# A gated recurrent layer with two steps in flight, and cosine attention in two token halves with its routing

## The reference

```python
x = x + cosine_attention(_layernorm(x), ...)   # 8 heads of 8, LayerNorm again inside, q and k scaled to length 1
x = x + moe(_layernorm(x), ...)                # 160 experts, 8 per token, and a shared one
x = x + gated_recurrent(_layernorm(x), ...)
x = x + moe(_layernorm(x), ...)                # the same weights
# then a state-space layer, a mixing layer, rotary attention and the mixing layer again

# gated_recurrent, for norm_inp = rmsnorm(inp, ln_w):
beta = sigmoid(norm_inp @ Wg.T)
hx_hat = norm_inp @ Wc.T
hx = scan over time of  h = (1 - beta) * h + beta * hx_hat
h_norm = rmsnorm(hx, ffn_w)
out = hx + (silu(h_norm @ w1.T) * (h_norm @ w3.T)) @ w2.T
```

## Time and profile before

| | before |
|---|---|
| runs, us | 3164.58, 3166.40, 3166.65 (median 3166.4) |
| profiled execution, us | 3175.44, its span 3173.6 |
| TensorE, VectorE, ScalarE, GpSimd busy, us | 1657.7, 1390.8, 958.2, 1066.0 |
| share of the chain that ended last: TensorE, issue, VectorE, unknown queue, ScalarE | 31%, 18%, 17%, 17%, 12% |
| mean granted TensorE clock | 0.704 of full |

### The profile page before, as it was taken

The page is one execution under the profiler, slowest core; times in us unless marked ns, Lnnn a source line. Parts: engine busy times, 40 slices in busy tenths (PEclk is TensorE's granted clock), DMA queues, the critical chain, the costliest instruction groups (busy, mean ns, idle before and its releaser), DMA issues.

```text
span 3173.6 us, 40197 instructions
## 1 busy us (share of the span) xinstructions
PE 1657.7 (52%) x13844; PEld 1113.4 (35%) x13844; DVE 1390.8 (44%) x3634; ACT 958.2 (30%) x1731; POOL 1066.0 (34%) x1177
## 2 busy tenths in 40 slices
PE   4763113229466633423333294656322456988985
PEld 2552112117344411311222173444211443454454
DVE  3548223213133444744442131334443466676655
ACT  3640000015222312111200042223258833344344
POOL 1003753640344265266336503452562020000001
PEclk9975555559777855555555597778665776898998
DMA  8991111339577611011013296767110000000000
GB/s 243 273 346 35 52 38 50 121 114 380 197 236 221 230 44 38 19 62 41 22 49 118 100 360 210 243 219 247 42 44 20 1 0 1 1 1 1 1 2 28
DMA packets 276792, 352.95 MB, mean 111 GB/s; under 512 B 68624, under 2 KB 161104, under 8 KB 276432
## 3 DMA queue, kind: packets, MB, share of 16 engines
q10 hardware_dynamic: 83984, 153.13, 13.8%
q1 hardware_dynamic: 159840, 130.08, 13.5%
q0 software_dynamic: 32768, 67.17, 6.8%
HBM read 201.35 MB, written 167.51 MB: 116 GB/s over the span
## 4 chain that ended last, share of the span: by engine, by line
PE 31%; issue 18%; DVE 17%; another core or an unknown queue 17%; ACT 12%; DMA 3%; SPq 1%; POOL 1%; ACTq 0%; DVEq 0%; POOLq 0%
ACT arena L1043 5%; PE psum L2159 5%; PE psum L2149 4%; PE psum L2110 4%; PE psum L448 3%; DMA arena<-expert_blocks 2%; PE psum L1494 2%; PE psum L1475 2%; PE psum L432 1%; PE psum L427 1%; ACT arena L1345 1%; PE psum L1491 1%; DVE X L1909 1%; PE psum L1492 1%
## 5 line engine op out<-in xcount | busy, mean ns | idle before, releaser
L1939 POOL DMA_INDIRECT arena<-slot_results,SLOTS x512 | 489.1, 955 | 729.0 <-DMA slot_results<-arena 326.5
L1928 POOL DMA_INDIRECT slot_rows<-arena,SLOTS x512 | 502.4, 981 | 522.2 <-issue 437.2
L1893 DVE COPY arena<-psum 128x512 f32<-128x512 f32 x288 | 195.7, 689 | 827.9 <-remote 521.3
L2149 PE MATMUL psum<-arena 128*64 128x128 f32 x2304 | 224.7, 324 | 299.4 <-issue 288.8
L1982 ACT ACTIVATE arena<-psum 128x512 f32<-128x512 f32 x288 | 172.0, 597 | 679.1 <-remote 304.6
L2159 PE MATMUL psum<-arena 64*128 64x128 f32 x2304 | 239.8, 335 | 206.6 <-issue 130.3
L2159 PEld LDWEIGHTS psum<-arena 64*128 64x128 f32 x2304 | 178.9, 218 | 269.4 <-issue 200.2
L2149 PEld LDWEIGHTS psum<-arena 128*64 128x64 f32 x2304 | 144.9, 158 | 362.8 <-issue 347.3
L2110 PE MATMUL psum<-ident,arena 128*128 128x128 f32 x1152 | 223.1, 325 | 15.7 <-DMA arena<-slot_rows 14.0
L169 POOL TENSOR_SCALAR rstd<-mv 128x4 f32<-128x4 f32 x32 | 6.8, 212 | 637.7 <-DVE mv L581 637.4
L1909 DVE SCALAR_TENSOR_TENSOR X<-arena,WEIGHTS,X 128x128 f32<-128x128 f32 x512 | 179.6, 352 | 27.9 <-DVE X L1909 5.9
(11 more groups left out here) (252 smaller groups left out, 3120.8 us busy)
## 6 DMA issues: line engine op xcount, KB each, us to landing
arena<-slot_rows ACTq DMA_DIRECT2D x288, 256.0 KB
slot_results<-arena ACTq DMA_DIRECT2D x288, 256.0 KB
arena<-expert_blocks SPq DMA_DIRECT2D x512, 96.0 KB
slot_rows<-zeros SPq DMA_DIRECT2D x2, 18432.0 KB, 79.9
arena<-own_blocks SPq DMA_DIRECT2D x44, 256.0 KB
slot_rows<-arena,SLOTS POOLq DMA_INDIRECT x512
arena<-slot_results,SLOTS POOLq DMA_INDIRECT x512
expert_blocks<-in_expert_w SPq DMA_DIRECT2D x1, 7680.0 KB, 26.1
```

Source lines behind the costliest of these rows:

```text
L1893: dve.tensor_copy(YSB[:, p].rearrange("p (c h) d -> p h c d", h=2), psum[:, first:first + 2, 0:256].rearrange("p h (c d) -> p h c d", c=2) ...
L1928: pool.indirect_dma_start(out=slot_rows[h], out_offset=bass.IndirectOffsetOnAxis(ap=slots_of(t, k), axis=0), in_=XNH[:, t], in_offset=None ...
L1939: pool.indirect_dma_start(out=GATHERED[:, n % TPI, k], out_offset=None, in_=slot_results[h], in_offset=bass.IndirectOffsetOnAxis(ap=slots_ ...
L2149: mm = pe.matmul(psum[lo:lo + INTER, 2 + 5 * (p % 2), o:o + P], gate_of(g, q), XSBT[:, p % 2, P * q:P * q + P], start=True, stop=True, ski ...
```

## The change

It has two parts. In the first, the attention runs in two halves of 16 tiles (4 steps each), and each half is followed by its routing: attention 0, routing 0, attention 1, routing 1. So the dispatch of half 0 stands beside the second half of the attention. For that the steps are written out (no loop), the barrier between the layers is gone, the padded copies and the inverse deviation move from GpSimd to VectorE (with ScalarE's Sqrt), the buffers lie elsewhere, and the first buffer is cleared ahead of the copies of the expert weights, the second behind them, with a semaphore each. In the second part, the recurrent layer has two steps in flight: the scan of step i + 1 and the front of step i + 2 stand ahead of step i's gates. The root mean square is no longer a full 128x512 tile but four columns (L660's reciprocal becomes one of 4 columns); `ffn_w` is multiplied into the weights once, the two products with W1 and W3 become eight of 128x128 that take the state itself, and a transposition and a copy are added. Sigmoid becomes Tanh and Abs, Sigmoid times its argument becomes Silu. The row sums are distributed anew.

```diff
         def middle_vector(dve):
...
-            own_tiles(dve)
             for h in range(HALVES):
+                cos_vector(dve, 0, HSTEPS * h, HSTEPS * h + HSTEPS)
+                if h == 0:
+                    own_tiles(dve)
+                dve.wait_ge(loaded_all, 16 * (len(weights) - FIRST_WEIGHTS))
                 route_half(dve, 0, h, nothing)
                 slots(dve, 0, h)
...
-        SUMS = ((0, 1), (2, 3, 4), (5, 6), (7, 8, 9))
+        SUMS = ((0,), (1, 2), (3, 4), (5,))
+        ROUTE_SUMS = ((6, 7), (8, 9), (10,), (11, 12))
...
                 for t in range(TPI):
                     place(dve, 1, t)
                 rows_of_slots(dve, 1, 0)
-                glru_front(dve, GLRU_AHEAD, 0)
-                for i in range(GLRU_AHEAD, STEPS):
-                    glru_vector(dve, i, 0, i < STEPS - 1, places(i))
+                sum_rows(dve, TILES - 3, 0)
+                glru_vector(dve, GLRU_AHEAD, STEPS, 0, places)
...
         def middle_gpsimd(pool):
 
-            pool.wait_ge(cleared, 16 * HALVES)
             for run in range(2):
                 for h in range(HALVES):
+                    pool.wait_ge(cleared[h], 16)
                     dispatch(pool, run, h)
...
+            def scan(i):
+                dve.wait_ge(g_beta.sem, g_beta.at(0, i))
+                dve.scalar_tensor_tensor(BETA, BETA, 1.0, psum[:, 2, :], ALU.add, ALU.mult).then_inc(g_hx.sem, 1)
+                dve.wait_ge(g_hx.sem, g_hx.at(0, i, 1))
+                dve.wait_ge(g_y.sem, g_y.before(0, i - 1))
...
+            for i in range(first, first + 2):
+                stats_of(i)
+                scale(i)
+            scan(first)
+            for i in range(first, last):
+                if i + 2 < last:
+                    stats_of(i + 2)
+                root(i)
+                if i + 2 < last:
+                    scale(i + 2)
+                if i + 1 < last:
+                    scan(i + 1)
+                between(i, 0)
+                gates(i)
+                between(i, 1)
+                add(i)
+                between(i, 2)
...
+        def glru_scalar(act, first, last):
...
+            spread(first)
+            tokens(first)
+            spread(first + 1)
+            beta(first)
+            for i in range(first, last):
+                if i + 1 < last:
+                    tokens(i + 1)
+                squares(i)
+                if i + 2 < last:
+                    spread(i + 2)
+                root(i)
+                if i + 1 < last:
+                    beta(i + 1)
+                gates(i)
+                turned(i)
...
+        def glru_tensor(pe, first, last, between):
...
+            for i in range(first, last):
+                up(i)
+                squares(i)
+                if i + 1 < last:
+                    project(i + 1)
+                between(i, 0)
+                if i + 2 < last:
+                    front_tensor(pe, i + 2, GLRU)
+                between(i, 1)
+                turn(i)
+                results(i)
+                between(i, 2)
```

More of the change, by code:

```diff
@@ L199, in program @@
         OT = view([P, SEQ])
+        assert used[0] <= GLRU_AT + 7 * W
+        used[0] = GATHER_AT
+        Qs = view([P, 32, HROWS], BF16)
+        Ks = view([P, 32, HROWS], BF16)
+        VP = view([P, 2, TPI, 8, 32])
         a_link = signal("a_link", 6)
@@ L219, in program, with cos_vector, stats_of, scale @@
         a_x = signal("a_x")
-        def cos_vector(dve, layer):
-            def front(s):
+        def cos_vector(dve, layer, begin, end):
+            def stats_of(s):
                 front_stats(dve, s, layer)
+            def scale(s):
+                invert(dve, s, layer)
                 front_scale(dve, s, layer)
@@ L284, in step @@
                 divide(i)
-            front(0)
-            squares(0)
-            normal(0)
-            front(1)
-            keys(0, 0)
-            squares(1)
-            front(2)
-            step(0, 0, first=True)
-            step(1, 1)
-            with dve.Fori(1, STEPS // 2 - 2) as i2:
-                for u in range(2):
-                    step(i2 * 2 + u, u)
-            for i in range(STEPS - 4, STEPS):
-                step(i, i % 2, left=STEPS - 1 - i)
-            add(STEPS - 1)
-            dve.wait_ge(a_x.sem, a_x.end(0))
+                if left >= 2:
+                    padded(i + 2)
+            dve.wait_ge(constants, CONSTANTS + 3)
+            stats_of(begin)
+            scale(begin)
+            stats_of(begin + 1)
+            squares(begin)
+            padded(begin)
+            normal(begin)
+            scale(begin + 1)
+            stats_of(begin + 2)
+            keys(begin, begin % 2)
+            squares(begin + 1)
+            padded(begin + 1)
+            for i in range(begin, end):
+                step(i)
+            add(end - 1)
+            dve.wait_ge(a_x.sem, a_x.at(0, end - 1))
         def psum_b16(bank):
@@ L453, in weigh_values, with cos_tensor @@
             return mm
-        def cos_tensor(pe, layer):
-            pe.wait_ge(constants, 17)
+        def cos_tensor(pe, layer, begin, end):
+            pe.wait_ge(constants, CONSTANTS + 3)
             def project(s):
@@ L508, in output, with step @@
                 mm.then_inc(a_y.sem, 1)
-            def step(i, u, first=False, left=STEPS):
+            def step(i):
+                u, left = i % 2, end - 1 - i
                 scores(i, u, 0)
                 scores(i, u, 1)
-                if not first:
+                if i > begin:
                     output(i - 1)
@@ L529, in step @@
                 values(i, u, 3)
-            front_tensor(pe, 0, layer)
-            project(0)
-            pe.wait_ge(a_qkv.sem, a_qkv.at(0, 0))
-            transposes(0)
-            front_tensor(pe, 1, layer)
-            pe.wait_ge(a_qt.sem, a_qt.at(0, 0))
-            pe.wait_ge(a_kt.sem, a_kt.at(0, 0))
-            project(1)
-            step(0, 0, first=True)
-            step(1, 1)
-            with pe.Fori(1, STEPS // 2 - 2) as i2:
-                for u in range(2):
-                    step(i2 * 2 + u, u)
-            for i in range(STEPS - 4, STEPS):
-                step(i, i % 2, left=STEPS - 1 - i)
-            output(STEPS - 1)
+            front_tensor(pe, begin, layer)
+            project(begin)
+            pe.wait_ge(a_qkv.sem, a_qkv.at(0, begin))
+            transposes(begin)
+            front_tensor(pe, begin + 1, layer)
+            pe.wait_ge(a_qt.sem, a_qt.at(0, begin))
+            pe.wait_ge(a_kt.sem, a_kt.at(0, begin))
+            project(begin + 1)
+            for i in range(begin, end):
+                step(i)
+            output(end - 1)
         def earlier(layer):
@@ L1656, in program @@
         JUNK2 = view([P, GROUP, NE], BF16)
-        XNH = view([P, TILES, D])
         EXT = view([P, W])
@@ L1672, in program @@
         GATHERED = view([P, TPI, TOPK, D])
-        cleared = semaphore("cleared")
+        cleared = [semaphore(f"cleared{h}") for h in range(HALVES)]
         blocked = semaphore("blocked")
-        stays = semaphore("stays")
         e_stat = signal("e_stat", HTILES, HALVES)
@@ L2285, in middle_tensor @@
             experts(0)
-            for i in range(GLRU_AHEAD):
-                glru_tensor(pe, i, nothing)
+            glru_tensor(pe, 0, GLRU_AHEAD, nothing)
             pe.wait_ge(g_link.sem, g_link.at(0, GLRU_AHEAD - 1))
@@ L2321, in barriers @@
         def barriers(layers):
-            return sum(k not in ("moe", "glru") for k in LAYERS[:layers])
+            return sum(k not in ("cos", "moe", "glru") for k in LAYERS[:layers])
         def finish(eng, layer):
             eng.drain().then_inc(phase_done, 1)
-            if layer == 0:
-                eng.wait_ge(loaded_all, 16 * (len(weights) - FIRST_WEIGHTS))
             eng.wait_ge(phase_done, ENGINES * barriers(layer + 1))
```

384 lines of the change are left out of this document (199 added, 185 removed).

## The result

The changed kernel takes 3192.8 us in the median of 14 runs (3170.7 to 3204.5), the kernel before 3166.5 us (14 runs): the ratio is 1.0068 [1.0051, 1.0085]. By this ratio it is slower by some 21 us (the two medians are 26 us apart); forecast were 3123 us. The profiled execution took 3176.76 us (span 3174.9), near the low end of its runs.

The account below looks back on a forecast made before the run. The front half was taken as bound by hand-offs between engines, slowed beside long indirect-DMA streams. Terms +5 - 36 - 12 = -43 us took the profiled 3175.4 to 3132, less 9 for the median: 3123; range 3070 to 3164.

Parts of the forecast that it names:

- rival A: Beside the streams: each hand-off is charged, not each microsecond, so the change is slower, 3180 us; chance 0.17.
- I take 0.25, nearest to routing: Beside a long DMA stream, work goes at 0.25 of its free pace; the ends are 0.04 and 0.49.
- the held stretch: Part of a long indirect-DMA stream, after some 40 free us to its end, where increments are held back.
- the prediction's own formula (546.2 - 126.4 e): Start of the second half's first dispatch, e being the pace beside the stream: 514.6 at 0.25, +5 us.
- a stream gives about 40 free us: In every long indirect-DMA stream, neighbours work freely for about 40 us and are slowed from there to its end.
- Steps 0 to 3 and 4 to 7: Recurrent layer beside gather and dispatch: 115 and 178.8 us, terms -36 (with moved row sums) and -12.
- The step of 18 us: Recurrent layer with two steps in flight: a free step takes 18 us with hand-offs, against 28.1 before.
- rival D: Recurrent layer: a new step takes 25 us, not 18, for 3151 to 3179 us; chance 0.13.
- A pause of 16 us gives the 40 back: In the streams: when GpSimd pauses for 16 us, its neighbours again get 40 free us.
- Everything behind is the same; 0: Both expert runs and the second layer have the same instructions, so their time changes by 0.
- the padded copies at nothing: Attention step: copies and reciprocal added on VectorE lie in its waits, priced 0, at most 3 us in each of 8 steps.
- rival C: First dispatch: VectorE's copies keep GpSimd from issuing, lengthening the stream by at most 16 us, 3139; chance counted within the forecast's 0.55.

Follow-up runs that it names:

- the four grains: Changed kernel with GpSimd pauses of about 5.5, 17, 33 and 10 us after each 8, 24, 32 and 16 DMAs in its four dispatches; 0.9748 holding, 1.0627 not.
- The halves' kernel: Attention and routing in halves, with the recurrent layer and row sums of the kernel before; ratio to before 0.983 not holding, 1.0063 holding.

## Why the prediction was wrong

It forecast faster by 43 us and the kernel is slower by 21; the time lies outside the range (3070 to 3164), and rival A (3180, chance 0.17) is what happened.

**The step that failed** is "I take 0.25, nearest to routing": a pace per microsecond for work in the held stretch. What counts there is each increment that is waited for. ScalarE's own come 1.40 us apart, and those of TensorE came 11.2 to 56.0 us apart in the rows above. An attention step has 15 increments of TensorE where a routing step has 5, and the held stretch let 7 through in 125 us against 7 to 10, so the pace that routing had could not be carried over. From the dispatch at 529.6 the prediction's own formula (546.2 - 126.4 e) gives e = 0.13; the term came out at +20 instead of +5. The sign that the prediction gave for A, no attention step finished by 374, is what the profile shows. That it is the count of increments is read from these profiles; no run changes the count alone.

**A second step failed: "a stream gives about 40 free us".** The first dispatch does. In the dispatch at 1362.0 only 20 us were free instead of the 38 of the sum, in all five profiles with the new recurrent layer and no pauses in that dispatch, and some 38 with the old one in the three others on holding chips. Two things differ there: the new layer has more increments in less time, and the gather ahead of that dispatch ended 11 us before it instead of 37. No run parts the two.

**Steps 0 to 3 and 4 to 7.** The step of 18 us was right (17.7), rival D wrong. Forecast were 115 and 178.8 us, measured 136.4 and 175.9. The second agrees by luck: half of the free time at the start was missing, and the stream I had drawn as unbroken pauses twice (19.3 and 24.7 us), since held steps bring their slots late. What I had at 0 was the routing behind: the stream's last 24 DMAs fell on it, +19.6 us, and behind steps 0 to 3 it grew by 17.5 where I had 12. Terms: -36 came out as -10, -12 as +5. With 0.13 in all three terms the sum would still have been -9 us (+20, -32, +3); the rest lies in steps 0 to 3 and in what comes behind.

**"A pause of 16 us gives the 40 back"** did not hold for pauses made of clears beside the attention: 17 us give 15. It had been read from one place of the trace of before, and the pause of 19.3 us in the changed kernel gives 30 there.

**"Everything behind is the same; 0"** is wrong twice. In the first experts 9 of the 20 us came back: the recurrent layer begins at 1109.3 instead of 1097.7. And most profiles of after end some 20 us later than the first: they differ in how many of 510 hand-offs fall into the held stretch and cost 1.40 instead of 0.33 us.

**Right:** the first dispatch near 208 (201.6); the padded copies at nothing; rival C wrong, with the stream at 167 us beside the copies on either kind of chip. The Trainium skill, page SBUF — State Buffer, section Who interferes with whom, says that copy and cast in a 2-port mode lock GpSimd out; by that the stream could have grown, and the traces do not show it (128 DMAs from 201.6 to 367.4). Also right were all durations that hold nothing: on chips that do not hold, the changed kernel gains 94 us.

What stays open: why some chips hold and others don't, what the account is made of, and what sets the length of a free stretch. The records fit a turn of about 0.7 us per semaphore change, 16 x 0.7 = 11.2 being the unit of the distances read above; this is arithmetic, and no run isolates it. That the grain of 5.5 us everywhere would gain more than the four grains was not tried.

## What to carry to other kernels

Before work is moved beside a long stream of indirect DMAs, count its hand-offs, not its microseconds, and look at what its neighbours did there: in the first dispatch, on a holding chip, short pauses of GpSimd (5.5 us after each 8 indirect DMAs) were worth more than they cost; on the other chips, where GpSimd's stream is the bound, pauses only cost. Time a change on more than one chip: the same diff was 1.007 on one kind and 0.963 on the other, and the kernel with four grains of pauses 0.975 and 1.063. A stage is called unchanged only when several profiles of it say so.

## What the runs showed of the hardware that was not expected

Chips of one type differ by 28% on one program (2479 against 3171 us). The halves' kernel begins its first dispatch at 202 us on either kind, and is 707 us apart at the last gather (1697.7 and 2404.8) and 755 at the end. So nearly all of the difference is in the stages with indirect DMAs; the last 48 us are in the chain of hand-offs behind the gather (785.4 against 737.6 us). On the slower ones 1.5 semaphore changes per us are recorded once the first dispatch is 30 to 40 us old, against 14.4 on the others with the same DMAs, and 36 on the same chip without indirect DMAs. How long a stream stays free is not fixed: 20 to 40 us were seen at the dispatches. The delay outlasts the stream: after the last DMA at 2418.0 the pitch of ScalarE's chain stays at 1.40 us until 2426.65.
